# A four-part transformer block on one core: the gates of eight experts spread to SBUF ahead, their sum moved to GpSimd

## The reference

```python
h = x @ down_w + down_b
probs = jax.nn.softmax(x @ router_w + router_b - COST_LAMBDA * cost, axis=-1)
topv, topi = jax.lax.top_k(probs, 2)
gate = jax.nn.softmax(topv, axis=-1)
for k in range(2):
    mask = jax.nn.one_hot(topi[..., k], 8, dtype=h.dtype)
    acc = jnp.zeros_like(h)
    for e, (w1, b1, w2, b2) in enumerate(expert_params):
        hm = h * mask[..., e:e + 1]
        acc = acc + (gelu(gelu(hm) @ w1 + b1) @ w2 + b2)
    out = out + acc * gate[..., k:k + 1]
out = out + 0.1 * (gelu(gelu(h) @ shared_w1 + shared_b1) @ shared_w2 + shared_b2)
out = out @ up_w + up_b + (gelu(x) @ core_w + core_b)
```

## Time and profile before

| what | value |
|---|---|
| runs | 455.63, 461.21, 461.37 us, median 461.21 |
| the profiled execution's own time | 461.77 us |
| its span, first to last instruction | 459.7 us |
| mean granted TensorE clock | 0.929 |
| busy PE / DVE / ACT / POOL | 401.3 / 255.9 / 208.7 / 94.4 us |

### The profile page before, as it was taken

One profiled execution on the slowest core, in us unless ns is written; L12 is line 12 of the kernel. 1 busy time (PEld: TensorE's weight loads), 2 busy tenths in 40 slices (PEclk: granted clock), 3 DMA queues, 4 the chain that ended last, 5 costly groups with the idle time before them and its releaser, 6 DMA issues.

```text
span 459.7 us, 9356 instructions
## 1 busy us (share of the span) xinstructions
PE 401.3 (87%) x3736; PEld 307.4 (67%) x3736; DVE 255.9 (56%) x650; ACT 208.7 (45%) x409; POOL 94.4 (21%) x173
## 2 busy tenths in 40 slices
PE   3688789989987889789899999999999778896996
PEld 2467568877875657466578887776788545664664
DVE  7878953355369575868923456782134566145222
ACT  2664372112224446646344447466322336847452
POOL 6833022313311023022002241000123220010000
PEclk9868769999998757999899999999999959999999
DMA  9990000000000000000000000000000000000000
GB/s 181 376 360 5 0 1 1 0 0 2 1 0 1 3 1 1 1 2 1 1 24 4 0 0 1 2 1 2 25 1 1 0 0 2 3 1 1 23 1 23
DMA packets 8218, 12.16 MB, mean 26 GB/s; under 512 B 4464, under 2 KB 6768, under 8 KB 7408
## 3 DMA queue, kind: packets, MB, share of 16 engines
q1 hardware_dynamic: 6880, 10.75, 7.1%
q10 hardware_dynamic: 1296, 0.82, 0.9%
HBM read 10.52 MB, written 1.05 MB: 25 GB/s over the span
## 4 chain that ended last, share of the span: by engine, by line
PE 61%; DVE 17%; issue 8%; ACT 8%; POOL 5%; POOLq 0%; DVEq 0%; ACTq 0%
PE Y L1128 21%; PE H L1128 16%; PE S L1128 14%; PE S L1169 3%; PE S L1229 2%; ACT A L685 2%; DVE MN L885 2%; DVE PT L886 2%; PE S L1193 1%; PE S L1136 1%; DVE K L872 1%; PE S L1202 1%; ACT L685 1%; DVE MN L892 1%; ACT PT L586 1%
## 5 line engine op out<-in xcount | busy, mean ns | idle before, releaser
L1128 PE MATMUL Y<-WP,A 128*128 128x256 f32 x256 | 61.2, 382 | 2.3 <-POOL A L774 2.3
L1013 DVE TENSOR_TENSOR R<-H,HH 128x512 f32<-128x512 f32 x32 | 22.1, 691 | 70.9 <-ACT HH L659 70.8
L1128 PE MATMUL H<-XT,WF 128*128 128x256 f32 x256 | 61.0, 383 | 0.0
L774 POOL TENSOR_TENSOR A<-R 128x512 f32<-128x512 f32 x32 | 33.5, 1048 | 133.1 <-DVE R L1013 133.1
L685 ACT ACTIVATE A<-H,B 128x256 f32<-128x256 f32 x84 | 38.5, 475 | 42.4 <-PE H L1128 42.2
L1128 PE MATMUL Y<-A,W 128*128 128x256 f32 x168 | 51.5, 419 | 4.6 <-ACT A L685 3.2
L1128 PEld LDWEIGHTS Y<-WP,A 128*128 128x128 f32 x256 | 47.5, 190 | 10.2 <-POOL A L774 2.1
L1128 PE MATMUL H<-GH,W 128*128 128x256 f32 x168 | 48.3, 400 | 4.9 <-ACT GH L676 4.3
L1128 PEld LDWEIGHTS H<-XT,WF 128*128 128x128 f32 x256 | 47.3, 190 | 7.8 <-issue 1.7
L659 ACT ACTIVATE HH<-H 128x512 f32<-128x512 f32 x32 | 19.1, 597 | 72.2 <-PE H L1128 72.2
L1128 PEld LDWEIGHTS H<-GH,W 128*128 128x128 f32 x168 | 32.2, 198 | 10.7 <-issue 6.2
(11 more groups left out here) (181 smaller groups left out, 655.8 us busy)
## 6 DMA issues: line engine op xcount, KB each, us to landing
W<-in_w SPq DMA_DIRECT2D x2, 1344.0 KB, 14.6
WF<-in_wf SPq DMA_DIRECT2D x2, 1024.0 KB, 12.4
WP<-in_wp SPq DMA_DIRECT2D x2, 1024.0 KB, 14.5
X<-in_x SPq DMA_DIRECT2D x8, 128.0 KB, 12.0
out_dram<-X SPq DMA_DIRECT2D x8, 128.0 KB, 1.7
CD<-in_ctx_in SPq DMA_DIRECT2D x2, 256.0 KB, 9.7
C<-in_ctx_in SPq DMA_DIRECT2D x1, 256.0 KB, 3.5
CT<-in_ctxT SPq DMA_DIRECT2D x1, 256.0 KB, 6.3
```

Source lines behind the costliest of these rows:

```text
L774: nc.gpsimd.tensor_tensor(flat(A0[:, n % 2, :, :]), R0[:, n % 2, :], R0[:, n % 2, :], ALU.mult).then_inc(a0_ready, 1)
L1013: nc.vector.tensor_tensor(R0[:, n % 2, :], b[:, :], HH[:, n % 2, :], ALU.max).then_inc(done, 1)
L1128: return nc.tensor.matmul(o, a, b, start=start, stop=stop, skip_group_check=shared)
```

## The change

The gates become stages of their own, `gb` 0 to 3, each for two experts: two matmuls fill one S bank (L1380 before, now in `spread_gates`), and ScalarE copies the 128x512 to SBUF (`broadcast_gates`), into the buffer HH that F's body uses for something else. There is room for four experts, so `gb` 2 and 3 wait until the second expert of the pair they overwrite has been taken out. `y` of an expert has two steps now: one VectorE instruction reads the result from PSUM, adds the negated zero row and multiplies by the gate; GpSimd adds to ACC. The semaphore `acc_step` counts the adds. The planner's table says `y="dve .45 pool .75"` in place of `y="act .45 dve 1.1"`, and has a new entry for `gb`. So the whole list is planned anew; up to `B3x` in the body of group 0 it is the same as before, from there on it differs.

```diff
@@ ffn1_down
-            out.append(("ffn1", g, "g", 0))
+            out += stages("ffn1", g, "g", "gb*2")
         if c == CH1[e] - 1:
             out.append(("ffn1", g, "y", EXPERTS.index(e)))
+            if e in (1, 3):
+                out.append(("ffn1", g, "gb", (e + 3) // 2))
@@ COST
-                e="act .11 dve 1.59", t="act .18 dve 7.59", d="pe .59 act 1.18", g="pe 1.43 act .24",
-                c="pe .43 act .33", w="pe .41", y="act .45 dve 1.1", o="pe 2.59 dve .09", b="act .1",
+                e="act .11 dve 1.59", t="act .18 dve 7.59", d="pe .59 act 1.18", g="pe 1.43 act .24", gb="pe .25 act .6",
+                c="pe .43 act .33", w="pe .41", y="dve .45 pool .75", o="pe 2.59 dve .09", b="act .1",
@@ chains_and_orders
+            order(("ffn1", g - 1, "y", E1), ("ffn1", g, "gb", 0))
@@ buffers
-        A1, YS, YG = A0[:, :, 0, :], HH[:, :, 0:GT], R0[:, :, 0:GT]
+        A1, YG = A0[:, :, 0, :], R0[:, :, 0:GT]
+        GB = HH[:, :, :].rearrange("p t (e s) -> p (t e) s", s=GT)
@@ ScalarE
-                if j > 2:
-                    read_out(act, "ffn1", g, "y", j - 2)
-                e = EXPERTS[j]
-                nc.scalar.activation(YS[:, j % 2, :], b[:, 0:GT], ACT.Identity, bias=Y0n[:, e:e + 1]
-                                     ).then_inc(ys_ready, 1)
+            def broadcast_gates(g, j):
+                b, done = filled(act, "ffn1", g, "gb", j)
+                if j >= 2:
+                    read_out(act, "ffn1", g, "y", EXPERTS.index(2 * j - 3))
+                elif g:
+                    read_out(act, "ffn1", g - 1, "y", E1)
+                nc.scalar.copy(flat(GB[:, 2 * (j % 2):2 * (j % 2) + 2, :]), b[:, :]).then_inc(done, 1)
@@ GpSimd
+            def expert(g, j):
+                if j == 0:
+                    read_out(pool, "ffn1", g, "y", 0)
+                    return
+                read_out(pool, "ffn1", g, "y", j)
+                if j > 1:
+                    pool.wait_ge(acc_step, g * E1 + j - 1)
+                nc.gpsimd.tensor_tensor(ACC[:, :], ACC[:, :], YG[:, j % 2, :], ALU.add).then_inc(acc_step, 1)
@@ VectorE
-                dve.wait_ge(ys_ready, n)
-                b = at("ffn1", g, "y", j)
-                nc.vector.tensor_tensor(YG[:, j % 2, :], YS[:, j % 2, :], b[:, GT:2 * GT], ALU.mult
-                                        ).then_inc(free["Y", "dve"], 1)
-                read_out(dve, "ffn1", g, "y", j)
-                add = nc.vector.tensor_tensor(ACC[:, :], ACC[:, :], YG[:, j % 2, :], ALU.add)
-                if j < E1:
-                    link(add)
-                else:
-                    add.then_inc(acc_ready, 1)
+                b, done = filled(dve, "ffn1", g, "y", j)
+                e = EXPERTS[j]
+                read_out(dve, "ffn1", g, "gb", e // 2)
+                if n > 2:
+                    dve.wait_ge(acc_step, n - 2)
+                nc.vector.scalar_tensor_tensor(YG[:, j % 2, :], b[:, 0:GT], Y0n[:, e:e + 1], GB[:, e % 4, :], ALU.add, ALU.mult
+                                               ).then_inc(done, 1)
@@ TensorE, down1
-                    b, _ = claim(pe, *y)
-                    if e == EXPERTS[1]:
-                        read_out(pe, "ffn1", g, "g", 0)
-                    if e < E1:
-                        mm(b[:, GT:2 * GT], selG[:, e, :], GTT[:, :])
+                    claim(pe, *y)
+            def spread_gates(g, j):
+                b, done = claim(pe, "ffn1", g, "gb", j)
+                if j == 0:
+                    read_out(pe, "ffn1", g, "g", 0)
+                for i in range(2):
+                    ins = mm(b[:, i * GT:(i + 1) * GT], selG[:, 2 * j + i, :], GTT[:, :])
+                ins.then_inc(done, 1)
@@ TensorE, widen
-                    pe.wait_ge(acc_ready, g + 1)
+                    pe.wait_ge(acc_step, E1 * (g + 1))
```

More of the change, by code:

```diff
@@ L118 @@
 FILLS = {(part, s): "S" for part, names in (("attn0", "q k s p o n"), ("attn1", "kv k q s p o x w m n a r"),
-                                            ("ffn0", "x r"), ("ffn1", "x r g d z")) for s in names.split()}
+                                            ("ffn0", "x r"), ("ffn1", "x r g gb d z")) for s in names.split()}
 FILLS |= {("ffn0", "u"): "H", ("ffn0", "y"): "Y", ("ffn1", "c"): "H", ("ffn1", "y"): "Y", ("ffn1", "o"): "Y"}
@@ L407, in mixed_network @@
         BY_ACT = {("attn0", s) for s in "qpo"} | {("attn1", s) for s in "xqmpoa"}
-        BY_ACT |= {("ffn0", "x"), ("ffn1", "x"), ("ffn1", "g"), ("ffn1", "d"), ("ffn1", "c")}
+        BY_ACT |= {("ffn0", "x"), ("ffn1", "x"), ("ffn1", "g"), ("ffn1", "gb"), ("ffn1", "d"), ("ffn1", "c")}
         READERS = ("act", "dve")
@@ L507, in mixed_network @@
         gb1_ready = sem("gb1_ready")
-        ys_ready = sem("ys_ready")
-        acc_ready = sem("acc_ready")
+        acc_step = sem("acc_step")
         stored = sem("stored")
@@ L705, in _ @@
                      ("ffn1", "t"): top_exp, ("ffn1", "b"): gelu_biases, ("ffn1", "d"): inner,
-                     ("ffn1", "c"): hidden, ("ffn1", "y"): expert})
+                     ("ffn1", "c"): hidden, ("ffn1", "gb"): broadcast_gates, ("ffn1", "y"): expert})
         @block.gpsimd
@@ L813, in _ @@
             run({("attn0", "v"): first, ("attn1", "v"): norm("attn1"), ("ffn0", "v"): norm("ffn0"),
-                 ("ffn1", "v"): norm("ffn1"), ("attn1", "kv"): keys1, ("ffn1", "d"): biases, ("ffn0", "u"): square})
+                 ("ffn1", "v"): norm("ffn1"), ("attn1", "kv"): keys1, ("ffn1", "d"): biases, ("ffn0", "u"): square, ("ffn1", "y"): expert})
         @block.vector
@@ L1076, in expert @@
                 if j == 0:
-                    read_out(dve, "ffn1", g, "y", 0)
                     return
                 n = g * E1 + j
-                dve.wait_ge(ys_ready, n)
-                b = at("ffn1", g, "y", j)
-                nc.vector.tensor_tensor(YG[:, j % 2, :], YS[:, j % 2, :], b[:, GT:2 * GT], ALU.mult
-                                        ).then_inc(free["Y", "dve"], 1)
-                read_out(dve, "ffn1", g, "y", j)
-                add = nc.vector.tensor_tensor(ACC[:, :], ACC[:, :], YG[:, j % 2, :], ALU.add)
-                if j < E1:
-                    link(add)
-                else:
-                    add.then_inc(acc_ready, 1)
+                b, done = filled(dve, "ffn1", g, "y", j)
[5 more added lines that the diff above has]
+                                               ).then_inc(done, 1)
             def result_ffn1(g, k):
@@ L1408, in _ @@
                  ("ffn0", "d"): down0, ("ffn1", "x"): turn_rows("ffn1"), ("ffn1", "r"): route("ffn1", XT1, RW, E1),
-                 ("ffn1", "g"): turn_gates, ("ffn1", "d"): narrow, ("ffn1", "z"): zero_row, ("ffn1", "c"): up1,
+                 ("ffn1", "g"): turn_gates, ("ffn1", "gb"): spread_gates, ("ffn1", "d"): narrow, ("ffn1", "z"): zero_row, ("ffn1", "c"): up1,
                  ("ffn1", "w"): down1, ("ffn1", "o"): widen})
```

## The result

The changed kernel took **474.21 us** (median of 4 runs, 471.91 to 475.77), beside 461.29 for the kernel before on the same chip: a ratio of **1.031** (95% interval 1.025 to 1.037), slower. Forecast were 467.0, with 455 to 472. The profiled execution took 473.69 us, its span 471.9.

A forecast was written before the change was run, and what follows sets the result against it. TensorE was taken as the bound, so only its stops and half clock counted. Terms 1.7 + 1.0 + 2.8 - 0.5 + 0.4 - 0.2 = +5.2 on the profiled 461.77 us gave 467.0, range 455 to 472.

The forecast's parts named there:

- The prices of the steps: Per instruction: `y` on VectorE 484 ns, add on GpSimd 732 ns, gate copy on ScalarE 586 ns.
- 12 table loads: Sign on ScalarE: 12 table loads in place of 16, at 1.28 us each.
- the tail: ScalarE's step to last projection: 1.4 us for 1.51, gain 0.1 in each of the last two groups, -0.2.
- the last group's `gb`: Last group: four gate copies push in between Gelus on ScalarE; 0.4 us of stops allowed.
- The three places: End of group 0's body +1.7 us, start of group 1's body +2.8, two stops in group 2 -0.5.
- the term for the clock: Group 0: half clock after the stop ahead of w14, taken as +1.0 from between nothing and 4.5 us.
- the 3.60: Earlier trace: TensorE's 3.60 us stop at the head of group 2's body, said to have brought half clock.
- the 2.06 of the earlier trace: TensorE's 2.06 us stop near the end of group 2's body, for ScalarE's Gelu; cited as without half-clock sequel.
- The rival *Clock: Stops in group 0, perhaps group 1, drop the clock; 470.5 us for one drop, 475.0 for two; chance 0.22.
- Relief: VectorE gets far ahead, neither new wait comes, old stops go; 457.4 us, at best 452.8; chance 0.20.

The follow-up runs named there:

- e5: Changed kernel plus 22 extra matmuls that nobody reads (fillers), put where TensorE stands in the three bodies; 465.80 us, 1.015 against the kernel before.
- e8: Changed kernel with stages moved in its list: `y` 5 right behind w11, `B4x` behind c5, B4w behind w5; 468.89 us, 1.012.
- e1: Changed kernel with the stage list of the kernel before in all bodies, `gb` put in; 459.59 us, 0.997.
- e2: Kernel before, with its own three-step `y`, in the changed kernel's stage list without `gb`; 486.99 us, 1.057.
- e3: Changed kernel with the old stage list in the body of group 0 alone; 463.26 us, 1.006.
- e4: Changed kernel with the old stage list in the body of group 1 alone; 468.00 us, 1.017.
- e7: Changed kernel with the old stage list and ten unread matmuls in group 2, seven ahead of its first `c`, three ahead of `B6x`; 455.84 us, 0.991.
- e9: Kernel before plus ten unread matmuls in group 2, seven ahead of its first `c`, three ahead of `B6x`; 459.60 us, 1.000.
- e6: Changed kernel with the old stage list and the add to ACC on VectorE in place of GpSimd; 460.96 us, 1.000.
- e10: As e7, but the router's `e` and `t` of group 3 moved behind all Gelus of group 2; 457.49 us, 0.993.

## Why the prediction was wrong

**The prices of the steps were right**: 483, 731 and 586 ns, 12 table loads, the tail 0.17 us shorter (forecast 0.1), the last group's `gb` +0.2 (forecast 0.4).

**The three places were right, and so was the way to the first two.** In group 0 w14 was to start at 228.1 by the clock of the kernel before, 34.9 us into the body; it started at 35.4. In group 1 the XA transpose was to come 6.7 us into the body; it came at 6.7. The stops were shorter than forecast only because TensorE came to them later: 1.43 in place of 3.5 ahead of w14, 2.19 for 2.5. In group 1 all new waits come to 4.3 for 2.8. In group 2 one stop of 2.20 took the place of two, but the one for `G3x`, which I had not followed, grew by 1.0. As waits, the three bodies have +1.8, +4.3 and +0.2, 6.3 in all, where the terms were +1.7, +2.8 and -0.5, 4.0 in all.

**The step that failed is the term for the clock, +1.0, in group 0 alone.** Slower matmuls measured 2.2 us there, and 2.4 and 4.3 in the bodies of groups 1 and 2, for which the sum had nothing: 8.8 in all, of which the fillers of e5 give back 7.1. I argued that a long stop must come first (3.5 us, answered as the 3.60), and took the 2.06 of the earlier trace rows as a sign that stops of two microseconds are free. The rows at hand said otherwise: in the earlier trace rows the half clock of 221.66 follows a stop of 0.91. In the changed kernel the clock fell after stops of 0.76 to 0.95 us among short matmuls, after 2.19, after 1.07, after 1.99 and 2.20. The rival *Clock*, at 0.22, gave 475.0 for two drops in full; the kernel took 474.2. It had the right cause and the wrong condition, since "a stop of 3.5 us" was not needed and in e8, without the wait for `y` 5, most of the half clock stayed. That its number fits is luck: the clock fell in more places than two, and the waits were larger than its sum had them.

**Two causes, then, in numbers**: the new list (e1 to e4), and in it waits of 6.3 us and a slow clock of 8.8. Relief came where its rival had it, in body 0 (-3.3 in e1), but the new list took it back there and more.

The old list is 2.5 us longer in body 2 with the new `y` (1.3 with fillers in both, e7 against e9). 1.0 of it is the stop ahead of w14, 2.22 in e7 and 1.18 before, and ScalarE's rows show where it comes from. Before, the table load for the router's Exp starts right behind ScalarE's step of `y` 6 and is under way while VectorE still works on the logits; in e7 there is no such step, and the load waits for the logits:

```profile
413.44 1.28 ACT L650 ACT_TABLE_LOAD   x1
...
413.93 0.18 DVE L982 TENSOR_TENSOR lg_ffn<-lg_ffn,lmax_ffn 128x16 f32<-128x16 f32 x1
```

```profile
405.81 1.28 ACT L702 ACT_TABLE_LOAD   x1 [1.12 <-DVE lg_ffn L1047]
```

It is the same in e1 and e6 (1.12 us each) against e9 (none). So where the removed step stood, the load began early, and that is lost with it. Why the load stands behind the wait in one program and ahead of it in the other is not shown.

The Trainium skill, GPSIMD Engine Reference, section "Performance versus the Vector engine", would have kept the add on VectorE. The instruction is 731 ns on GpSimd against 425 on VectorE, a factor of 1.72; but e6 shows no loss by it, since GpSimd is idle and only the tail waits for it.

What stays open: what makes the clock fall after the same stop in one program and not in another (body 1 of e3 against that of the changed kernel).

## What to carry to other kernels

A cost table that orders a whole program is part of every edit to it: time the new steps in the old order, and the new order with the old steps, before judging either. Where TensorE is the bound, count each cluster of stops, short ones too, as a risk of half clock over the matmuls behind it. Its price is the work that follows without a wait; where a wait for another engine follows, slow matmuls only shorten that wait. If dependences can't be moved, matmuls that nobody reads, put into the idle time, can buy part of it back: 7.1 of 15 us here, and 0.9 us where a wait followed (e9).

## What the runs showed of the hardware

Stops under one microsecond each, with short matmuls between them, were followed by half clock: in the changed kernel 0.95, 0.76 and 0.91 us, then four matmuls in 2.08 us in place of 1.13 from 220.61 on; before, 0.67 and 0.91, then 1.96 from 221.66 on. With 8 extra matmuls the body stayed at 1.00 (e5).

A table load took 1.28 us, and the instruction behind it started 1.29 to 1.30 us after the load had (all but the first load, in the kernel before and the changed one). In e7 a load itself stood idle for 1.12 us until the input of its Exp was there; the same load began without a wait in the kernel before and in e9, behind another ScalarE step.

The same instructions up to the first body took 187.2 us in one execution and 192.5 in another; windows over them (e9, then e10) differ in the granted clock:

```profile
0.00:187.20 187.20, 148.19 (x1560) 118.83 (x1560) 122.99 (x290) 79.26 (x147) 56.72 (x114) 0.93 0.18 57
```

```profile
0.00:187.20 187.20, 154.34 (x1514) 123.97 (x1515) 118.97 (x272) 75.99 (x141) 56.72 (x114) 0.86 0.18 57
```

These 5 us are of the size of the spread of the kernel before (455.5 to 463.3 us in 23 runs), and as much as e7 gains: one execution of each would not have told it.
